# Attention output turned in 32x32 blocks on VectorE in place of TensorE transposes, in a gated cross-attention and expert kernel with a new step order

## Chip, cores and metric

One core of one Trainium2 chip. The metric is the device time of one execution in microseconds (us); lower is better. All times below are of the kernel before the change.

## The reference, cut to what matters

```python
def xattn(query, key, value):            # query = layernorm(x): 16 batches x 100 rows x 256
    Q, K, V = query @ Wq.T + bq, key @ Wk.T + bk, value @ Wv.T + bv   # key = value: 16 x 361 x 256
    # 16 heads of 16
    scores = softmax(einsum('bhsd,bhtd->bhst', Q, K) / sqrt(16))
    out = einsum('bhst,bhtd->bhsd', scores, V).reshape(B, 100, 256)
    return out @ Wh.T + bh

x = x + tanh(g_xattn) * xattn(layernorm(x), ctx, ctx)
x = x + tanh(g_ffn) * ffn(layernorm(x))  # RMS norm, gate with top 2 of 8 experts,
                                         # shared w1, w3, w2 with low-rank terms per expert
```

## The kernel before, in words

**Two phases.** The attention runs over the 16 batches in steps `i`; each `body(i)` is written out by hand once for every engine, and the engines meet only at semaphores. The expert part follows: 32 passes `g` (4 groups of 4 batches, 8 slices of 128 hidden columns). The last two attention steps, `late_step` (step 14) and `last_step` (step 15), have orders of their own, since the expert part's weights and first tokens are prepared in them. Every engine executes its list strictly in order, so a wait holds all that stands behind it in that list.

**One ordinary step, `body(i)`, on TensorE:**
- `s_head(i+1, h)`, 16 of them (L1270): scores of batch i+1 with the rows of the query on partitions, one head at a time, into two PSUM banks in turn. Each needs the maximum of head h-2 to be taken (`head`, VectorE, L985). The negated maxima go to `nmax`.
- `row_turn` and `second_rows` (L1276): the maxima of 8 heads turned to rows; ScalarE copies them to `crow` (`row_copy`, L513) and sends them (`row_send`, L517, a small DMA) into row 96 of the stack QS[b % 3]. That row, times ones in KS, subtracts the maximum inside the score matmul.
- `st_unit(i, u)`, 12 of them (L1293): transposed scores of batch i, keys on partitions, four heads in each unit, in three banks in turn; ScalarE's `expo(i, u)` (L525) takes the exponential to `pt`. Unit n needs exponential n-3. Units 0 to 5 need the first row transfer (`cr_a`), units 6 to 11 the second (`cr_b`).
- `k_part` (L1240) and `v_part` (L1252): K and V of batch i+2 as sums of high and low parts, in the two banks `pP`. ScalarE makes `k_high` and `v_out`, VectorE `k_low` (L818). SP and GpSimd send the K halves into the stacks KS (L244, L343).
- `pv_unit(i, u)`, 12 units of 4 matmuls (L1306), at the step's end: the share-weighted values and, by a column of ones in `va`, the sums. Head 4q+g goes to partitions 32g to 32g+16 and columns 100q to 100q+99 of the bank `pO`.

**What is done with `pO`, one step later.** ScalarE copies it to `osb` first thing in its `body` (L639; L681, L707 and L733 in the last steps). TensorE turns it with four 128x100 transposes (`o_turn`, L1314 to L1318) into `pP[1]`. VectorE takes the reciprocal of the sums (`shares`, L960) and multiplies (`quotient`, L966) into `on`. SP stores `on` to `o_dram` and loads it back as `xr` (L287, L294), which lays heads and rows out as the reference's reshape wants them; the bias of V goes the same way once, through `v_dram` (L290). In the next step TensorE turns `xr` (`on_turn`, L1330), VectorE copies it to `ot` (`turned_o`, L971), TensorE multiplies with Wh (`y_proj`, L1339) and VectorE adds to `xs` (`first_sum`, L976; `variance` follows, L823).

**Context.** GpSimd loads the context of batch i+4 into `craw` (`ctx_load`, L338), issues the q loads (`q_load`, L333), the low K stacks (`k_stack_low`, L343) and, after them, the low half of the context of batch i+3 (`ctx_low`, L328), for which ScalarE's `ctx_high_of(i+3)` (L471) must be done; then one of the expert weight loads (`late_load`, L354, steps 3 to 10: three of 512 KB, three of 256, one of 264, one of 128).

**Shared places.** `pP[1]` holds in turn the K half 0, `o_turn`'s result, the row turn of the first maxima, `on_turn`'s and `y_proj`'s results.

## Time and profile before

| | us |
|---|---|
| median of 3 runs | 501.02 (500.54 to 503.68) |
| the profiled execution | 504.5 |
| its span, first to last instruction | 502.6 |
| TensorE matmuls busy | 485.9 (97%) |
| TensorE weight loads busy | 455.5 (91%) |
| VectorE busy | 357.5 (71%) |
| ScalarE busy | 266.6 (53%) |
| GpSimd busy | 276.3 (55%) |

The profile is of one execution. PE is TensorE, PEld its weight loads, DVE VectorE, ACT ScalarE, POOL GpSimd, SP the engine that only issues transfers; an engine name with q behind it is that engine's issuing of DMAs. An instruction's row gives its start, duration, line, output and inputs; in brackets stands the idle time before it and what ended it. Starts of matmuls in a row show what each costs, their durations overlap.

### The profile page before, as it was taken

How to read it: one execution, taken by the hardware profiler on the slowest of the kernel's cores; microseconds unless marked ns; L12 is line 12 of the kernel's file. 1: busy time of each engine (PE TensorE's matmuls, PEld its weight loads, DVE VectorE, ACT ScalarE, POOL GpSimd, SP SyncE). 2: the span in 40 equal slices, each digit the busy share in tenths (PEclk: the TensorE clock that was granted, in tenths of full speed). 3: DMA queues.
4: the chain of work that ended last, by engine and by line, in shares of the span. 5: the costliest groups of instructions: out<-in, count | busy, mean ns of one | idle time of the engine just before them, and what ended most of it. 6: DMA issues, size and time to landing. Idle time of an engine off the chain costs nothing.

```text
span 502.6 us, 11753 instructions
## 1 busy us (share of the span) xinstructions
PE 485.9 (97%) x4350; PEld 455.5 (91%) x4350; DVE 357.5 (71%) x771; ACT 266.6 (53%) x584; POOL 276.3 (55%) x336
## 2 busy tenths in 40 slices
PE   7888999999999999999999999999999999999996
PEld 6656999999999999998999998999999999999994
DVE  6846787878778878987796879756476556764444
ACT  4446766676766666668866532534435423333331
POOL 5646555666666666566415437634396434844440
PEclk9979999999999999999999999999999999999999
DMA  6793686677767676554260000010000100001001
GB/s 204 179 291 90 198 209 150 151 202 204 199 172 177 161 168 161 126 121 94 29 206 9 1 0 2 1 34 0 1 1 1 34 1 1 0 2 34 0 1 33
DMA packets 51144, 45.83 MB, mean 91 GB/s; under 512 B 33935, under 2 KB 40115, under 8 KB 51088
## 3 DMA queue, kind: packets, MB, share of 16 engines
q1 hardware_dynamic: 41310, 23.18, 19.6%
q0 software_dynamic: 7504, 18.69, 14.1%
q10 hardware_dynamic: 2274, 3.21, 1.9%
q8 instruction: 35, 0.57, 0.5%
q14 instruction: 21, 0.17, 0.1%
HBM read 20.59 MB, written 6.66 MB: 54 GB/s over the span
## 4 chain that ended last, share of the span: by engine, by line
PE 87%; DMA 5%; DVE 4%; issue 1%; ACT 1%; POOL 1%; ACTq 0%; DVEq 0%
PE bank L1426 14%; PE bank L1270 8%; PE bank L1293 7%; PE bank L1306 7%; PE bank L1430 7%; PE bank L1443 7%; PE bank L1478 6%; PE bank L1252 6%; PE bank L1240 5%; PE bank L1458 4%; DMA QS<-crow 3%; PE bank L1339 3%; PE bank L1227 2%; PE bank L1461 2%; PE bank L1386 2%; DMA craw<-ctxT 2%
## 5 line engine op out<-in xcount | busy, mean ns | idle before, releaser
L985 DVE TENSOR_REDUCE nmax<-bank 100x1 f32<-100x361 f32 x256 | 129.9, 529 | 38.2 <-PE bank L1270 33.4
L419 POOL TENSOR_TENSOR awl<-hb,awh 128x400 fp32r<-128x400 f32 x63 | 71.2, 1132 | 119.8 <-ACT awh L623 119.8
L525 ACT ACTIVATE pt<-bank 120x400 f32<-120x400 f32 (+1 forms) x192 | 90.0, 501 | 24.1 <-PE bank L1293 11.1
L623 ACT ACTIVATE awh<-hb 128x400 fp32r<-128x400 f32 x64 | 34.5, 539 | 118.5 <-DVE hb L921 118.2
L1270 PE MATMUL bank<-KS,QS 96*100 96x362 f32 x256 | 87.0, 359 | 3.4 <-DVE nmax L985 3.1
L914 DVE TENSOR_TENSOR hb<-sil,bank 128x400 f32<-128x400 f32 x64 | 36.5, 570 | 71.4 <-PE bank L1443 36.8
L1293 PE MATMUL bank<-QS,KS 97*120 97x200 f32 (+1 forms) x384 | 66.3, 270 | 0.7 <-DMA QS<-crow 0.6
L328 POOL TENSOR_TENSOR cth<-craw,cth 128x724 fp32r<-128x724 f32 x16 | 27.6, 1728 | 64.8 <-ACT cth L471 55.2
L1293 PEld LDWEIGHTS bank<-QS,KS 97*120 97x120 f32 (+1 forms) x384 | 60.3, 184 | 1.9 <-DMA QS<-crow 1.5
L1270 PEld LDWEIGHTS bank<-KS,QS 96*100 96x100 f32 x256 | 41.7, 167 | 10.3 <-DVE nmax L985 3.7
L333 POOL DMA_DIRECT2D QS<-q_dram x90 | 46.0, 519 | 0.4 <-issue 0.3
L1252 PE MATMUL bank<-wkv,cth 128*120 128x256 f32 (+1 forms) x288 | 45.2, 286 | 0.0
L921 DVE TENSOR_TENSOR hb<-hb,wbT 128x400 f32<-128x400 f32 x64 | 43.2, 675 | 2.1
L1240 PE MATMUL bank<-cth,wkv 128*128 128x362 f32 x192 | 41.9, 330 | 0.8 <-POOL wkv L321 0.8
L343 POOL DMA_DIRECT2D KS<-kn x64 | 31.9, 508 | 16.1 <-DVE kn L818 10.4
L618 ACT ACTIVATE sil<-bank 128x400 f32<-128x400 f32 x64 | 31.5, 492 | 16.4 <-PE bank L1430 11.7
L1252 PEld LDWEIGHTS bank<-wkv,cth 128*120 128x120 f32 (+1 forms) x288 | 39.3, 183 | 0.3 <-issue 0.3
L1306 PE MATMUL bank<-pt,va 120*17 120x100 f32 (+1 forms) x1536 | 36.5, 249 | 0.0
L1306 PEld LDWEIGHTS bank<-pt,va 120*17 120x17 f32 (+1 forms) x1536 | 32.5, 97 | 3.8 <-issue 3.6
L1240 PEld LDWEIGHTS bank<-cth,wkv 128*128 128x128 f32 x192 | 32.7, 190 | 1.4 <-POOL wkv L321 1.4
L423 POOL TENSOR_TENSOR awsl<-aws,awsh 128x400 fp32r<-128x400 f32 x31 | 33.8, 1090 | 0.0
L502 ACT ACTIVATE va<-bank 120x256 f32<-120x256 f32 (+1 forms) x48 | 18.4, 383 | 8.4 <-PE bank L1252 8.2
(225 smaller groups left out, 1109.7 us busy)
## 6 DMA issues: line engine op xcount, KB each, us to landing
KS<-kn SPq DMA_DIRECT2D x128, 90.5 KB, 3.3
KS<-kn POOLq DMA_DIRECT2D x64, 90.5 KB, 3.4
craw<-ctxT POOLq DMA_DIRECT2D x14, 361.0 KB, 5.1
QS<-q_dram POOLq DMA_DIRECT2D x92, 50.0 KB, 3.5
q_dram<-qn ACTq DMA_DIRECT2D x4, 400.0 KB, 4.4
o_dram<-on SPq DMA_DIRECT2D x16, 100.0 KB
xr<-o_dram SPq DMA_DIRECT2D x16, 100.0 KB
y<-xs SPq DMA_DIRECT2D x8, 200.0 KB
```

Of the source, the lines that this page charges most:

```text
L333: pool.dma_start(QS[b % 3][row + DH * odd:row + DH * odd + DH, :, odd, :, :].rearrange("p g j s -> p g (j s)").bitcast(F32), src[odd]).the ...
L419: nc.gpsimd.tensor_tensor(awl[:, g % 2, slot], hb[:, slot], awh[:, g % 2, slot].bitcast(F32), ALU.subtract).then_inc(m["p_awl"], 1)
L525: nc.scalar.activation(pt[0:TW[t], u, :], pT[u % 3][0:TW[t], 0:CS], ACT.Exp, scale=float(DH) ** -0.5).then_inc(m["act_e"], 1)
L914: nc.vector.tensor_tensor(hb[:, slot], sil[:, slot], pU[1][:, 0:CS], ALU.mult).then_inc(m["d_hb"], 1)
L921: nc.vector.tensor_tensor(hb[:, slot], hb[:, slot], wbT[g // FT % 2][:, slot], ALU.mult).then_inc(m["d_aw"], 1)
L985: nc.vector.tensor_reduce(nmax[:, h // 8, pos % 8:pos % 8 + 1], pS[h % 2][0:S, 0:T], AX.X, ALU.max, negate=True).then_inc(m["dve_s"], 1)
L1240: last = mm(pP[(1, 0)[j]][:, 0:TP], wkv[:, 0, hw, k, j * 128:(j + 1) * 128], cth[:, b % 2, hc, k, :], start=p == 0, stop=p == 5)
L1252: last = mm(bank[0:TW[t], 0:D], cth[:, b % 2, hc, k, T0[t]:T0[t] + TW[t]], wkv[:, 1, hw, k, :], start=p == 0, stop=p == 5)
L1270: mm(pS[h % 2][0:S, 0:TP], QS[b % 3][0:96, g, h % 2, j, :], KS[b % 3][0:96, g, j, :], start=True, stop=True).then_inc(m["pe_s"], 1)
L1293: last = mm(pT[u % 3][0:TW[t], j * 2 * S:(j + 1) * 2 * S], KS[b % 3][:, q, j, T0[t]:T0[t] + TW[t]], QS[b % 3][:, q, :, j, :], start=True, ...
L1306: last = mm(pO[32 * g:32 * g + VW, q * S:(q + 1) * S], va[0:TW[t], b % 3, t, 4 * q + g, :], pt[0:TW[t], u, g * S:(g + 1) * S], start=t == ...
L1426: mm(pU[a][:, 0:CS], up_w[a][hw][:, j, fs], tt[hc][c % 2][:, j, :], start=t + j == 0, stop=False)
```

## The change

The bank `pO` is turned by one VectorE block transpose (each 32x32 block in its place) straight into `oT`: 13 blocks of 32 columns, so partitions 32g + (row in block), block c, and the 17 values of a head side by side. Head 4g+q now lies in group g. `shares` and `quotient` work on 128 partitions. `o_dram` has a layout by blocks, the loads into `xr` come in two halves (rows of even and odd start) over 104 rows, and `turned_o` puts the columns in order with two strided copies. `pO` and `xr` are filled once at the start. ScalarE's copies to `osb` and TensorE's `o_turn` are gone. The permutation of the columns of Wq and Wk follows. The order of the ordinary step and of steps 14 and 15 is new on TensorE, ScalarE and VectorE.

```diff
-        o_dram = nc.dram_tensor("o_dram", [B, H * S, DH], F32, kind="Internal").ap()
+        o_dram = nc.dram_tensor("o_dram", [B, OC, 128, DH], F32, kind="Internal").ap()      # OC = 13, RG = 26
-        osb = sba("osb", [128, NQ, S])
-        on = sba("on", [S, H, DH])
-        xr = sba("xr", [S, D])
+        oT = sba("oT", [128, OC, 32])
+        on = sba("on", [128, OC, DH])
+        xr = sba("xr", [4 * RG, D])
...
 SP, body(i)
-                    sp.dma_start(xr[:], o_dram[i - 1].rearrange("(r c) d -> r (c d)", c=H)).then_inc(m["xi"], 16)
+                    for half in range(2):
+                        sp.dma_start(xr[half * 4 * OC:(half + 1) * 4 * OC],
+                                     o_dram[i - 1].rearrange("c (g h p) d -> h g c (p d)", g=4, h=2)[half]).then_inc(m["xi"], 16)
...
 ScalarE, body(i)
-                if has_o(i):
-                    wait(act, "pe_pv", i * UN)
-                    wait(act, "pe_oT", i - 1)
-                    nc.scalar.activation(osb[:].rearrange("p q s -> p (q s)"), pO[:, 0:CS], ACT.Copy).then_inc(m["act_o"], 1)
+                if has_c(i):
+                    ctx_high_of(i + 3)
                 row_copy(i, 1)
                 row_send(i, 1)
+                k_high(b, 0)
                 expo(i, 0)
-                k_high(b, 0)
+                k_high(b, 1)
                 expo(i, 1)
-                k_high(b, 1)
                 expo(i, 2)
...
                 expo(i, 7)
+                expo(i, 8)
                 v_out(b, 1)
-                expo(i, 8)
+                row_send(i + 1, 0)
                 expo(i, 9)
-                row_send(i + 1, 0)
                 expo(i, 10)
                 expo(i, 11)
                 v_out(b, 2)
-                if has_c(i):
-                    ctx_high_of(i + 3)
...
 VectorE, start
             nc.vector.memset(nmax[:], 0.0).then_inc(m["nm_ok"], 1)
+            nc.vector.memset(pO[:, 0:OC * 32], 1.0).then_inc(m["pO_ok"], 1)
+            nc.vector.memset(xr[:], 0.0).then_inc(m["xr_ok"], 1)
...
+            def blocks_turned(i):
+                dve.wait_ge(m["pe_pv"], i * UN)
+                wait(dve, "dve_on", i - 1)
+                nc.vector.transpose(oT[:].rearrange("p c d -> p (c d)"), pO[:, 0:OC * 32]).then_inc(m["dve_o"], 1)
...
             def turned_o(i):
                 dve.wait_ge(m["pe_onT"], i)
-                nc.vector.tensor_copy(ot[:].rearrange("p k s -> p (k s)"), pP[1][:, 0:KT * S]).then_inc(m["dve_ot"], 1)
+                for half in range(2):
+                    nc.vector.tensor_copy(ot[:].rearrange("p k (g s) -> p k g s", g=4)[:, :, :, half:25:2],
+                                          pP[1][:, 0:KT * 4 * RG].rearrange("p (k h g c) -> p h k g c", k=KT, h=2, g=4)[:, half, :, :, 0:OC - half]).then_inc(m["dve_ot"], 1)
...
 VectorE, body(i)
                 head(i + 1, 0)
                 head(i + 1, 1)
+                if has_o(i):
+                    blocks_turned(i)
                 head(i + 1, 2)
...
                 k_low(b, 1)
+                head(i + 1, 6)
                 if has_o(i):
                     shares(i)
-                head(i + 1, 6)
                 head(i + 1, 7)
-                if has_o(i):
-                    quotient(i)
                 head(i + 1, 8)
                 head(i + 1, 9)
                 head(i + 1, 10)
                 head(i + 1, 11)
+                if has_o(i):
+                    quotient(i)
+                head(i + 1, 12)
+                head(i + 1, 13)
                 if has_y(i):
                     turned_o(i)
...
                 (variance and first_sum now stand here, before heads 14 and 15)
                 head(i + 1, 14)
                 head(i + 1, 15)
...
 TensorE
-            def o_turn(i):
-                ...
-                wait(pe, "act_o", i)
-                for q in range(NQ):
-                    last = nc.tensor.transpose(pP[1][0:S, q * 128:(q + 1) * 128], osb[:, q, :], ident[:])
-                last.then_inc(m["pe_oT"], 1)
...
 TensorE, body(i), b = i + 2, s = s_head(i + 1, .), st = st_unit(i, .), k and v in halves (a, b); the new order in full:
+  s0 s1 k0a k0b s2 st0 s3 k1a k1b s4 st1 s5 st2 st3 s6 st4 s7 st5 v0a st6 s8 v0b s9 row_turn st7 st8 s10
+  v1a s11 v1b st9 s12 st10 s13 st11 on_turn v2a s14 v2b s15 y_proj, then pv 0 to 11, second_rows
-  s0 st0 s1 k0a s2 k0b s3 k1a s4 st1 k1b s5 st2 o_turn st3 st4 s6 s7 st5 v0a v0b st6 s8 st7 s9 st8 row_turn
-  v1a s10 v1b on_turn s11 st9 st10 s12 v2a v2b s13 st11 y_proj s14 s15, then pv 0 to 11, second_rows
...
 late_step, last_step: o_turn out, blocks_turned in on VectorE; st_unit(B - 1, 0) and (B - 1, 1) with their
 exponentials move from last_step into late_step; on_turn(B - 1) comes first in last_step after gate(0);
 on_turn(B - 2) and y_proj(B - 2) come earlier; w_high and tokens_high on ScalarE, and masks, first_u,
 second_u, variance on VectorE, are put in a new order
```

## Rows read from the trace of the kernel before

**Rows 1.** The page, shares of the span in the chain that ended last, by engine
```profile
PE 87%; DMA 5%; DVE 4%; issue 1%; ACT 1%; POOL 1%; ACTq 0%; DVEq 0%
```
**Rows 2.** Windows by step: stretch, length, busy of PE, PEld, DVE, ACT, POOL, PEclk, DMA
```profile
178.01:191.25 13.24, 13.24 (x182) 12.57 (x186) 10.66 (x25) 8.99 (x22) 8.78 (x14) 1.00 0.74 179
...
sum 147.61, PE 146.91 PEld 138.44 DVE 118.81 ACT 99.27 POOL 94.44; mean PE 13.36 PEld 12.59 DVE 10.80 ACT 9.02 POOL 8.59
...
231.60:242.49 10.89, 10.89 (x160) 9.37 (x164) 9.46 (x24) 10.30 (x24) 7.39 (x5) 1.00 0.23 30
...
253.16:264.40 11.24, 11.24 (x150) 10.59 (x150) 10.37 (x19) 6.66 (x15) 2.67 (x2) 1.00 0.69 208
```
**Rows 3.** The chain in order of time, inside the step from 123.73
```profile
126.65 5.45 DMA QS<-crow
```
**Rows 4.** Windows, a stretch of the start
```profile
29.40:36.20 6.80, 6.46 (x14) 3.71 (x15) 1.81 (x4) 1.55 (x4) 5.04 (x10) 0.50 1.06 296
```
**Rows 5.** Timeline of TensorE in the quiet step: start, duration, line
```profile
180.14 0.25 PE L1276 MATMUL bank<-ident,nmax 100*8 100x100 f32 x1
...
181.44 0.66 PE L1240 MATMUL bank<-cth,wkv 128*128 128x362 f32 x3
181.94 0.33 PE L1270 MATMUL bank<-KS,QS 96*100 96x362 f32 x1
...
183.86 0.60 PE L1318 MATMUL bank<-ident,osb 128*100 128x128 f32 x4
184.22 0.66 PE L1293 MATMUL bank<-QS,KS 97*121 97x200 f32 x4
184.72 0.49 PE L1270 MATMUL bank<-KS,QS 96*100 96x362 f32 x2
...
185.25 0.89 PE L1252 MATMUL bank<-wkv,cth 128*121 128x256 f32 x6
185.97 0.36 PE L1293 MATMUL bank<-QS,KS 97*121 97x200 f32 x2
...
188.24 0.57 PE L1293 MATMUL bank<-QS,KS 97*121 97x200 f32 x4
188.65 0.33 PE L1270 MATMUL bank<-KS,QS 96*100 96x362 f32 x1
```
**Rows 6.** Timeline of ScalarE in the quiet step
```profile
180.27 0.50 ACT L639 ACTIVATE osb<-bank 128x400 f32<-128x400 f32 x1 [1.95 <-PE bank L1306]
...
180.93 0.63 ACTq L517 DMA_DIRECT2D QS<-crow  x1
...
182.14 0.56 ACT L496 ACTIVATE kn<-bank,bks 128x362 fp32r<-128x362 f32 x1
```
**Rows 7.** Groups by line, whole span: count | busy us, mean ns | idle before
```profile
L895 DVE TENSOR_TENSOR uth<-uTh,mk 128x800 fp32r<-128x800 f32 x4 | 6.5, 1618 | 0.1
...
L971 DVE COPY ot<-bank 128x200 f32<-128x200 f32 x17 | 6.1, 356 | 0.0
...
L950 DVE COPY fo<-bank 128x400 f32<-128x400 f32 x4 | 2.3, 575 | 2.0 <-PE bank L1514 1.7
```
**Rows 8.** Timeline of VectorE in the quiet step
```profile
182.76 0.59 DVE L818 SCALAR_TENSOR_TENSOR kn<-bank,bks,kn 128x362 fp32r<-128x362 f32 x1
...
185.08 0.97 DVE L985 TENSOR_REDUCE nmax<-bank 100x1 f32<-100x361 f32 x2
...
189.89 0.53 DVE L985 TENSOR_REDUCE nmax<-bank 100x1 f32<-100x361 f32 x1 [0.21 <-PE bank L1270]
```
**Rows 9.** Timelines of GpSimd and ScalarE at the start of step 4
```profile
112.39 0.73 POOL L354 DMA_DIRECT2D w<-w3T  x1
113.12 0.72 POOL L338 DMA_DIRECT2D craw<-ctxT  x1
...
113.22 0.63 ACTq L517 DMA_DIRECT2D QS<-crow  x1
```
**Rows 10.** Timeline of VectorE in the start
```profile
10.04 0.54 DVE L779 CAST cth<-craw 128x724 fp32r<-128x724 f32 x1 [1.76 <-DMA craw<-ctxT]
```

More of the change, by code:

```diff
@@ L1097, in late_step @@
                 head(B - 1, 6)
-                shares(B - 2)
                 head(B - 1, 7)
-                quotient(B - 2)
+                blocks_turned(B - 2)
                 head(B - 1, 8)
                 head(B - 1, 9)
+                turned_o(B - 2)
+                shares(B - 2)
+                head(B - 1, 10)
+                quotient(B - 2)
+                head(B - 1, 11)
                 tokens_low(0, 0)
-                head(B - 1, 10)
-                head(B - 1, 11)
-                turned_o(B - 2)
                 head(B - 1, 12)
@@ L1678, in late_step @@
                 st_unit(B - 2, 7)
-                on_turn(B - 2)
-                token_turn(0, 1)
+                y_proj(B - 2)
                 st_unit(B - 2, 8)
```

194 lines of the change are left out of this document (91 added, 103 removed).

## The prediction

> **What bounds the kernel.** Four views, in this order. First the shares of the chain that ended last: TensorE has 87% of it, a transfer 5%, VectorE 4% [rows 1]. So time comes off only where TensorE's own queue gets shorter or stops waiting. Second, the windows, one per ordinary step: a quiet step takes 13.24 us and TensorE is busy in all of it; VectorE has 10.66 us of work, ScalarE 8.99, GpSimd 8.78 [rows 2]. VectorE is therefore the next limit, at 81% of a step. The eleven steps from 70.20 to 217.81 sum to 147.61 us [rows 2], 1.97 more than eleven quiet ones (145.64). Third, the chain inside one of the long steps says what that excess is: TensorE waits for the small transfer that carries the negated maxima into QS (5.45 us from issue) [rows 3]. Fourth, the timelines of TensorE, VectorE and ScalarE inside the quiet step.
>
> **The profiled execution against the median.** It took 504.5 us, 502.6 of them span; the median of the runs is 501.02. The windows of the start show 6.80 us with the granted clock at 0.50, its lower level, with TensorE busy 6.46 us of them [rows 4]; at full clock that work would need about half, 3.2 us. That is nearly the whole difference of 3.5 us, so I take the median to be the same program without that stretch, work out differences in the profiled step and subtract them from 501.02.
>
> **Removed on TensorE: `o_turn`.** In the quiet step its four transposes start at 183.86 and the score units behind them at 184.22, so 0.36 us. Those four score matmuls then run to 184.72, 0.50 us, where the same four elsewhere need 188.24 to 188.65, 0.41 [rows 5]. The 0.09 more is the tail of the transposes. Price of one `o_turn`: 0.45 us. There are 16.
>
> **Removed on ScalarE: the copy to `osb`.** It starts at 180.27, and the send of the maxima is issued at 180.93, holding ScalarE 0.63 us [rows 6]. Without the copy the row copy starts when its transpose is done, about 0.24 us earlier, and so does the send.
>
> **Added on VectorE.** The block transpose, 416 elements from PSUM into SBUF. No such operation is in the trace. Nearest from below is the 128x200 copy at 356 ns; a copy of 128x400 from PSUM takes 575; the dearest pass over a similar tile is 1618 ns for 128x800 [rows 7]. I take 0.58, nearest in shape and source, and keep 0.36 and 1.62. The Trainium skill, "Vector Engine (DVE) Microarchitecture Reference", section 3.8, says the reorder array passes one element per cycle and lane when it transposes; with a clock of 0.96 GHz that is an estimate of 0.43 us for the stream alone, and no run here shows it yet. The reciprocal shrinks from 16 to 13 columns a partition and the quotient from 256 to 208: nothing much. `turned_o` becomes two strided copies of 104 and 96 columns for one of 200: between 0 and 0.36 more, I take 0.15. Together VectorE gets 0.6 to 0.7 us more a step, 11.3 of 13.
>
> **The new order of an ordinary step,** walked from its start R (the transpose of the second maxima), with starts from the timelines: a score head takes 0.17 us, a score unit 0.20, half a K projection 0.50 (181.44 to 181.94), half a V projection 0.36 (185.25 to 185.97 is two) [rows 5]; VectorE starts heads 0.44 apart when they wait for nothing (two in 0.97, one lasting 0.53), and a `k_low`, 0.59 long, holds it 0.5 by the same overlap [rows 8]. R is 180.14 in the quiet step.
> - The transpose sits behind head 1, from R+1.33. Head 2 comes only after a whole K projection, with its maximum ready to start at R+1.79, and head 4 at R+3.34, so the transpose is hidden up to about 0.7 us of duration. It costs TensorE nothing at 0.58. Behind it on VectorE queue all heads, and TensorE's heads wait two heads back, so beyond 0.7 us everything shifts.
> - K high 1 on ScalarE (0.56 us [rows 6]) now stands before exponential 1; its projection's last matmul starts before R+2.97, and 0.3 later its bank can be read, so it ends at R+3.83 and frees ScalarE 0.09 before that. Exponential 1 ends at 4.24, and score unit 4, which needs its bank, would start at 4.09: 0.18 late. Unit 5 is 0.07 late behind exponential 2. Head 9 needs maximum 7, which VectorE ends at R+5.95: TensorE is there at 5.95 by then. So some 0.27 us of waits, at one place.
> - Further on nothing waits by more than 0.05. The order of now has some 0.1 us of small gaps of its own, around `y_proj` and the last two heads (an estimate: what the quiet step's 13.24 has over the sum of its parts at these spacings); heads 14 and 15 now stand ahead of `y_proj`, so I let them go.
> Sum: 13.24 - 0.45 + 0.27 - 0.10 = 12.96, so 0.28 less, 13 steps: **3.6 us**.
>
> **The transfer of the maxima.** Two changes pull against each other. Score unit 6, which waits for the second half, moves up from R+5.83 to R+5.27, while the send moves up only by 0.24; In the quiet step the send is issued at R+0.79; with the 5.45 us of the long step it lands at R+6.24 now and at R+6.00 after, and unit 6 would wait 0.7 us for it. But what stands ahead of it moves too: GpSimd issues a 512 KB weight load at 112.39 and the 361 KB context load at 113.12, just as the maxima are sent at 113.22 in that step [rows 9]. In the new order ScalarE makes the high half of the context one batch ahead, so GpSimd's `ctx_low` no longer waits for it; it runs after the K low stacks, and the two big loads leave about 3.5 us before R. The maxima then find the queues emptier. From 164.78 on, where those loads are small or over, the same transfer lands in time already. I count 1.6 of the 1.97 us as gained: **1.6 us**.
>
> **Steps 14 and 15 and the first expert pass** hold three more `o_turn`, 1.35 us. Step 14 (231.60 to 242.49) is 10.89 us with VectorE at 9.46 and ScalarE at 10.30 [rows 2]; there the transpose isn't hidden and two exponentials and two score units of step 15 come in, which step 15 loses again. I take 0.5 off: **0.85 us**. In the expert pass (253.16 to 264.40) the transpose delays VectorE's products by 0.5, but TensorE is busy in all 11.24 us of it [rows 2], so it has work in hand: nothing, at worst 0.5. **Start:** two memsets more on VectorE, which later sits idle 1.76 us for the first context [rows 10]: nothing; at worst 0.7, since a tile of 400 columns costs 0.58 [rows 7] and the other memset is smaller. **SP:** eight small loads of `xr` in step 0 in place of one, and two a step after; all are issued in stretches in which SP has only its waits: nothing. The quotient comes later (after head 11), and its store still leaves behind the K stacks as now: `on_turn` of the next step waits for neither.
>
> **Total:** 3.6 + 1.6 + 0.85 = 6.05. From the profiled execution 504.5 - 6.05 = 498.45; from the median 501.02 - 6.05 = 495.0.
>
> **Rivals.**
> - *Clean gain.* TensorE waits nowhere new: 16 x 0.45 + 1.97 + 13 x 0.05 = 9.8, so 491.2. For it: ScalarE and VectorE are not full. Against: the waits above come out of the order itself. Chance 0.15.
> - *VectorE takes over in the first half of the step.* Each of its operations would hold it for longer than the heads' spacing shows, for instance the transpose and the two strided copies by 0.3 us more each way; ordinary steps then gain only about 0.05: 495.0 + 13 x 0.23 + 0.5 = 498.5. Against it: heads that last 0.53 us start 0.44 apart [rows 8]. Chance 0.13. The Trainium skill, "VectorE: DVE Perf Modes", section "The DRAIN you can't avoid", states that after every operation the pipeline is flushed for about its duration less 266 ns, and advises to keep the number of operations low; by that rule a transpose of 0.58 would hold VectorE for 0.89, and the trace disagrees, since a head is followed by the next before its own end.
> - *The maxima land too late.* If their transfer keeps its 5.45 us, unit 6 waits 0.7 in the six steps with a weight load: 495.0 + 6 x 0.7 + 0.3 = 499.5. For it: the unit moved up more than the send. Chance 0.14.
> - *The block transpose is dear, and the kernel slower.* Place: behind head 1, with all of the step's maxima behind it. Up to 0.7 us it is free, and above that each 0.1 us costs 0.1 in 13 ordinary steps and 2 others. The 6.05 are used up at 0.7 + 6.05/15 = 1.1 us. At 1.62 us [rows 7] it is 495.0 + 15 x 0.92 = 508.8. For it: it moves data across lanes, and none of the rows does. Chance 0.08.
> - *The change doesn't do what it says,* the reordering giving as much away as `o_turn` frees: 501 less the transfers, 499 to 501. It is in the chances of the second and third rivals.
>
> **How the numbers follow.** The forecast, with its own range 493 to 498, has 0.50. About 1% (5 us) is what a measurement of this kernel tells from no change. Faster by more (below 496.0): most of the forecast's 0.50 (0.42) and the clean gain's 0.15, 0.57. Slower (above 506.0): most of the last case, 0.08. Between: 0.35. The range reaches from 490.5, a little under the clean gain, to 501.0, which holds the second and third rivals and leaves the dear transpose out.
>
> **What would show it.** A block transpose of 0.5 to 0.65 us; L1318 gone; quiet steps near 12.96; the step's first waits on TensorE at score units 4 and 5 for ScalarE; no or hardly a wait for the maxima's transfer in the chain, GpSimd's context load before R; VectorE near 11.3 us a step. It is wrong if quiet steps stay at 13.2 (then look at VectorE between heads 4 and 9), if the transfer's share of the chain stays at 3% or more, or if the transpose lasts over 0.7 us. The clock may also fall elsewhere in the start, which is worth up to 3 us in a single run and nothing on the change.

## The result and the profile after

The changed kernel takes 511.88 us (median, 510.03 to 514.25) against 502.31 us for the kernel before on the same chip (500.54 to 503.68): ratio 1.0199, 95% interval 1.0161 to 1.0238. The forecast was 495.0 us, in a range of 490.5 to 501.0; the time came out 16.9 us above it, and slower than before. The profiled execution took 511.96 us, 510.2 of them span. Here and below a ratio counts only executions in the chip's faster state while a median counts all of them, which matters for two of the runs.

The page of the kernel after: busy times, and the chain that ended last by engine and by line.
```profile
PE 485.0 (95%) x4286; PEld 450.4 (88%) x4286; DVE 373.6 (73%) x806; ACT 253.5 (50%) x568; POOL 276.1 (54%) x336
...
PE 79%; DVE 14%; issue 3%; ACT 2%; DMA 1%; DVEq 0%; ACTq 0%
```
TensorE's share of the chain fell from 87% to 79% and VectorE's rose from 4% to 14%; the transfers went from 5% to 1% [rows 1]. So the transfers did leave the chain, as forecast, and VectorE took their place.

Windows of the kernel after, by step, with the columns of rows 2. Each window begins at the first product of probabilities and values, which closes one step, and is named here after the step that follows it; the last two rows are steps 12 and 13.
```profile
83.15:97.10 13.95, 13.46 (x175) 12.31 (x174) 11.81 (x26) 8.16 (x21) 8.58 (x15) 1.00 0.70 173
...
180.73:194.68 13.95, 13.48 (x175) 12.32 (x174) 11.79 (x26) 8.15 (x21) 8.23 (x14) 1.00 0.70 160
...
208.62:223.09 14.47, 13.70 (x176) 12.37 (x175) 13.21 (x33) 7.52 (x20) 7.55 (x13) 1.00 0.52 116
223.09:238.21 15.12, 13.72 (x177) 12.71 (x177) 14.08 (x33) 8.30 (x21) 6.18 (x11) 1.00 0.46 104
```
The ten ordinary steps from 69.23 to 208.62 are all alike, 13.92 to 13.95 us, where the quiet one was 13.24 [rows 2]. The eleven from 69.23 to 223.09 add up to 153.86 us, 6.25 more than the 147.61 before. TensorE is no longer busy in all of a step: 13.48 of 13.95.

Where in the step it is lost, the timelines of VectorE, GpSimd and TensorE say (start, duration, line; three fences, one engine each).
```profile
176.09 1.06 DVE L988 TENSOR_REDUCE nmax<-bank 100x1 f32<-100x361 f32 x2
177.06 1.35 DVE L967 TENSOR_TENSOR on<-oT,rz 128x208 f32<-128x208 f32 x1
178.34 0.96 DVE L988 TENSOR_REDUCE nmax<-bank 100x1 f32<-100x361 f32 x2
```
```profile
176.41 1.76 POOL L337 TENSOR_TENSOR cth<-craw,cth 128x724 fp32r<-128x724 f32 x1
178.09 0.56 POOL L363 DMA_DIRECT2D ag<-agT  x1
```
```profile
178.92 0.41 PE L1280 MATMUL bank<-KS,QS 96*100 96x362 f32 x1 [0.49 <-DVE nmax L988]
```
The quotient lasts 1.35 us and ends at 178.41, just after GpSimd's `ctx_low` (to 178.17). The maxima of heads 12 and 13 come behind it, and TensorE waits for them at head 14. The groups by tile say that this is the rule.
```profile
L958 DVE STREAM_TRANSPOSE oT<-bank x16: 605/606/616, 58.4 to 266.7; 128x416 f32<-128x416 f32 x16
L962 DVE RECIPROCAL rz<-oT x16: 220/230/241, 62.2 to 267.3; 128x13 f32<-128x13 f32 x16
L967 DVE TENSOR_TENSOR on<-oT,rz x16: 355/1349/1376, 66.4 to 267.6; 128x208 f32<-128x208 f32 x16
```
Minimum, median and maximum in ns: the quotient needs 355 where GpSimd computes nothing beside it, and 1349 in the median. The block transpose is 606 ns, as forecast.

The last steps lose in the same way. VectorE in steps 13 and 15 of the kernel after, and GpSimd beside the second group:
```profile
223.60 0.77 DVE L842 SCALAR_TENSOR_TENSOR rt<-rt,scl 100x8 f32<-100x8 f32 x1
224.40 0.65 DVE L844 SCALAR_TENSOR_TENSOR scl<-rt,scl 100x8 f32<-100x8 f32 x1
...
253.31 0.98 DVE L967 TENSOR_TENSOR on<-oT,rz 128x208 f32<-128x208 f32 x1
...
255.03 1.52 DVE L866 TENSOR_TENSOR dm<-top 100x4 f32<-100x4 f32 x1
```
```profile
252.76 1.30 POOL L411 TENSOR_TENSOR a2l<-a,a2h 128x512 fp32r<-128x512 f32 x1 [0.75 <-ACT a2h L599]
254.01 2.51 POOL L411 TENSOR_TENSOR w2l<-w,w2h 128x1024 fp32r<-128x1024 f32 x1
```
A multiplication of 100x8 takes 0.77 us and a difference of 100x4 1.52. Two windows, the first of the kernel after, the second of the kernel before, show what stands behind the last product's start:
```profile
259.11:505.46 246.35, 243.53 (x1463) 235.48 (x1462) 162.16 (x303) 98.64 (x201) 121.11 (x103) 1.00 0.05 17
```
```profile
253.09:497.87 244.78, 243.25 (x1467) 235.98 (x1466) 160.34 (x297) 99.11 (x203) 121.86 (x103) 1.00 0.05 16
```
That is 1.57 us more. With the eleven steps (+6.25), the start and first step (-0.97) and the three steps between (+0.7) it makes the 7.6 us by which TensorE ends later in the two profiled executions (505.46 against 497.87). The medians lie 9.6 apart. Most of the rest is the clock in the start: the profiled execution of before has 6.8 us at the granted clock of 0.50 there [rows 4], that of after 3.4 (30.30 to 33.71), and half of the difference, 1.7 us, is my estimate of what that lent the kernel after; so the -0.97 isn't a gain of the change.

### The profile page after: what moved, and what is told of

It reads as the page before. It is cut to its first block, busy times and chain, and to the rows that moved or that the text cites. A ratio compares the mean times of both kernels' runs of the same rounds, so it can differ in the third digit from the quotient of the medians.

```text
span 510.2 us, 11653 instructions
## 1 busy us (share of the span) xinstructions
PE 485.0 (95%) x4286; PEld 450.4 (88%) x4286; DVE 373.6 (73%) x806; ACT 253.5 (50%) x568; POOL 276.1 (54%) x336
## 4 chain that ended last, share of the span: by engine, by line
PE 79%; DVE 14%; issue 3%; ACT 2%; DMA 1%; DVEq 0%; ACTq 0%
PE bank L1425 13%; PE bank L1280 8%; PE bank L1429 6%; PE bank L1477 6%; PE bank L1303 6%; PE bank L1442 6%; PE bank L1316 6%; PE bank L1250 5%; PE bank L1262 4%; PE bank L1457 4%; DVE nmax L988 3%; DVE on L967 3%; PE bank L1338 3%; PE bank L1237 3%; PE bank L1460 2%
## 5 line engine op out<-in xcount | busy, mean ns | idle before, releaser
L988 DVE TENSOR_REDUCE nmax<-bank 100x1 f32<-100x361 f32 x256 | 126.8, 521 | 22.2 <-PE bank L1280 19.1
L534 ACT ACTIVATE pt<-bank 120x400 f32<-120x400 f32 (+1 forms) x192 | 83.9, 504 | 6.5 <-PE bank L1303 6.5
L1303 PE MATMUL bank<-QS,KS 97*120 97x200 f32 (+1 forms) x384 | 68.0, 273 | 1.0 <-DMA QS<-crow 1.0
L1303 PEld LDWEIGHTS bank<-QS,KS 97*120 97x120 f32 (+1 forms) x384 | 58.4, 184 | 3.7 <-DMA QS<-crow 1.2
L1262 PE MATMUL bank<-wkv,cth 128*120 128x256 f32 (+1 forms) x288 | 50.9, 289 | 0.0
L919 DVE TENSOR_TENSOR hb<-hb,wbT 128x400 f32<-128x400 f32 x64 | 44.3, 692 | 2.1
L1262 PEld LDWEIGHTS bank<-wkv,cth 128*120 128x120 f32 (+1 forms) x288 | 42.3, 182 | 0.5 <-issue 0.3
L1250 PE MATMUL bank<-cth,wkv 128*128 128x362 f32 x192 | 37.4, 330 | 0.0
L505 ACT ACTIVATE kn<-bank,bks 128x362 fp32r<-128x362 f32 x32 | 17.9, 562 | 24.4 <-PE bank L1250 24.4
```

Source lines behind the costliest of these rows:

```text
L534: nc.scalar.activation(pt[0:TW[t], u, :], pT[u % 3][0:TW[t], 0:CS], ACT.Exp, scale=float(DH) ** -0.5).then_inc(m["act_e"], 1)
L919: nc.vector.tensor_tensor(hb[:, slot], hb[:, slot], wbT[g // FT % 2][:, slot], ALU.mult).then_inc(m["d_aw"], 1)
L988: nc.vector.tensor_reduce(nmax[:, h // 8, pos % 8:pos % 8 + 1], pS[h % 2][0:S, 0:T], AX.X, ALU.max, negate=True).then_inc(m["dve_s"], 1)
L1250: last = mm(pP[(1, 0)[j]][:, 0:TP], wkv[:, 0, hw, k, j * 128:(j + 1) * 128], cth[:, b % 2, hc, k, :], start=p == 0, stop=p == 5)
L1262: last = mm(bank[0:TW[t], 0:D], cth[:, b % 2, hc, k, T0[t]:T0[t] + TW[t]], wkv[:, 1, hw, k, :], start=p == 0, stop=p == 5)
L1303: last = mm(pT[u % 3][0:TW[t], j * 2 * S:(j + 1) * 2 * S], KS[b % 3][:, q, j, T0[t]:T0[t] + TW[t]], QS[b % 3][:, q, :, j, :], start=True, ...
```

## The experiments

Theory A, from these rows: VectorE's operation with SBUF operands only is held while GpSimd reads SBUF; the quotient came into that place because its input moved from PSUM to SBUF, and because `ctx_low` and the quotient now fall together. Rival: the quotient is slow by itself (its strided view of 13 groups of columns, or the order it stands in). The Trainium skill, "SBUF — State Buffer", section "🔬 SBUF: two separate sides", states the rule: VectorE and GpSimd share a pair of ports under an exclusive lock, a VectorE operation with two SBUF inputs competes for it with a GpSimd operation that reads SBUF, and whichever starts first holds it for its whole instruction while the other waits. By that rule the quotient would end after `ctx_low`, which the rows above show (178.41 and 178.17).

**Take the overlap away, in three ways.** GpSimd's low half before its stacks of k; the quotient behind head 7; ScalarE's high half back at the end of its step.
```diff
 # e1_low_first, GpSimd
+                if i >= -1 and has_c(i):
+                    ctx_low(i + 3)
                 if i >= 0 and has_k(i):
...
                     k_stack_low(i + 2)
-                if i >= -1 and has_c(i):
-                    ctx_low(i + 3)
 # e2_quotient_early, VectorE
                 head(i + 1, 7)
+                if has_o(i):
+                    quotient(i)
...
                 head(i + 1, 11)
-                if has_o(i):
-                    quotient(i)
 # e3_high_back, ScalarE
-                if has_c(i):
-                    ctx_high_of(i + 3)
                 row_copy(i, 1)
...
                 v_out(b, 2)
+                if has_c(i):
+                    ctx_high_of(i + 3)
```


> Only edit to the changed kernel: GpSimd makes the low half of the context (ctx_low, 1.76 us) before the K low stacks of the same step, so at about 1 to 3 us of the step in place of 7.4 to 9.2, where VectorE's quotient stands. Theory A (the quotient, whose two inputs now both lie in SBUF, is held while that GpSimd pass runs): the quotient falls from 1.35 us to 0.36 in every step, quiet steps from 13.94 to 12.9 to 13.0, the whole from 511.9 by 11 to 12 us to about 500. Rival B (the quotient is slow by itself where it stands, or VectorE is simply full in the new order, so that another operation takes its place as the last one): quiet steps stay at 13.7 or more, the whole above 508.

> Only edit to the changed kernel: VectorE's quotient stands behind head 7 in place of head 11; GpSimd's queue is as in the changed kernel, so at that time it issues the K low stacks and the low half of the context has not begun. Theory A: the quotient takes 0.36 us there, although GpSimd issues transfers beside it; it adds 0.3 us to the maxima that bind between heads 7 and 9, so quiet steps come to 13.0 to 13.3 and the whole to 500 to 504. Rival B (any work of GpSimd beside it, issuing transfers too, holds it): it stays above 0.8 us, quiet steps stay at 13.7 or more, the whole above 508.

> Only edit to the changed kernel: ScalarE makes the high half of the context at the end of the step and not one batch ahead, as in the kernel before. GpSimd's low half then waits for it and runs at the end of the step, and the weight and context loads stand beside the send of the maxima again. Theory A: the quotient takes 0.36 us; quiet steps (with small loads) about 12.95. For the maxima's transfer I expect TensorE to wait for it in the steps 3 to 7, by 0.3 to 0.7 us each, so the whole is 2 to 4 us above the run with the low half first: 502 to 504. Rival B: quotient 1.35, the whole above 508. If the transfer wait is absent, the whole equals that of the run with the low half first within 1 us.

Measured: 519.9 us (ratio 1.0346, 1.0285 to 1.0407), 510.31 (1.018, 1.0126 to 1.0233) and 520.32 (1.0351, 1.029 to 1.0412). The quotient's group in the second, then its longest one:
```profile
L967 DVE TENSOR_TENSOR on<-oT,rz x16: 353/359/2429, 62.7 to 265.6; 128x208 f32<-128x208 f32 x16
```
```profile
132.14 2.43 DVE L967 TENSOR_TENSOR on<-oT,rz 128x208 f32<-128x208 f32 x1 [1.19 <-DMA o_dram<-on]
```
In all three the median is 0.36 or 0.37 us and an undisturbed step 13.09 to 13.17. The hold is gone from the ordinary step, theory A stands for the quotient and its rival falls. The one long quotient of the second run says the same: it came late, since it had to wait for the store before it, fell beside `ctx_low` (132.61 to 134.33) and lasted until 134.57. But the time didn't come back. My totals (500, 500 to 504, 502 to 504) missed by 6 us and more and lie where I had put the rival, and two of the runs are slower than the changed kernel. Who waits for a transfer, and windows of the first:
```profile
PE bank L1329 <- DMA xr<-o_dram: 7.5, 5, 2.4
```
```profile
170.41 8.20 DMA o_dram<-on
```
```profile
169.70:187.07 17.37, 14.48 (x175) 12.79 (x174) 10.91 (x26) 8.29 (x21) 12.18 (x20) 0.94 0.90 176
```
and of the third:
```profile
PEld bank L1303 <- DMA QS<-crow: 6.0, 5, 2.0
```
```profile
110.14:128.43 18.29, 16.47 (x176) 15.37 (x175) 11.10 (x26) 8.32 (x21) 8.92 (x14) 0.81 0.64 140
```
TensorE waits five times for `xr` in the first run, where the store of the quotient takes 7 to 9.4 us to land before the longest waits, and five times for the maxima in the third. In a step like the last row the granted clock falls to 0.81 in the mean: 18.29 us are 13.1 plus 1.8 of waiting plus 3.4, which is half of a stretch of 6.8 us at the lower level, 1.2 GHz, that follows the wait. Theory B, then: with steps of 13.1 us two transfers come too late where GpSimd's large loads (weights and context) are issued ahead of them, and a wait of TensorE can cost a stretch at 1.2 GHz besides. That the held quotient hid this, since steps of 13.94 us leave the transfers more time, is my reading and no run tests it alone; in the last run of this document, with steps of 13.94 us too, TensorE still waits twice for `xr` (3.1 us).

**A control in the kernel before**, for the other side of theory A: same collision, but the quotient reads PSUM.
```diff
 # e5_psum_beside: the kernel before
             def body(i):
                 b = i + 2
+                if has_c(i):
+                    ctx_high_of(i + 3)
...
                 v_out(b, 2)
-                if has_c(i):
-                    ctx_high_of(i + 3)
 # VectorE
                 head(i + 1, 7)
-                if has_o(i):
-                    quotient(i)
                 head(i + 1, 8)
                 head(i + 1, 9)
+                if has_o(i):
+                    quotient(i)
```


> A control in the kernel before, for the duration of one instruction and not for the time: ScalarE makes the high half of the context one batch ahead, so GpSimd's low half follows the K low stacks, and VectorE's quotient (here with one input in PSUM, one in SBUF) stands behind head 9, where that GpSimd pass runs. Theory A (only an operation whose two tensor inputs are both in SBUF is held): the quotient keeps its 0.41 us in all steps although GpSimd's pass lies over it. Rival (any VectorE operation that touches SBUF is held): 1 us or more in the steps where they overlap.

VectorE and GpSimd in that run:
```profile
62.98 0.41 DVE L966 TENSOR_TENSOR on<-bank,rz 100x256 f32<-100x256 f32 x1
```
```profile
62.84 1.74 POOL L328 TENSOR_TENSOR cth<-craw,cth 128x724 fp32r<-128x724 f32 x1
```
All 16 quotients take 0.41 or 0.42 us. But the control is weaker than planned: in 11 of the 13 steps in which the two overlap, the quotient starts 0.08 to 0.13 us ahead of `ctx_low`, where being first could save it anyway. Only this one and the one at 256.51 start inside GpSimd's operation, and they aren't held. The kernel before has the case more often, at the end of its steps (GpSimd, then VectorE):
```profile
178.41 1.72 POOL L328 TENSOR_TENSOR cth<-craw,cth 128x724 fp32r<-128x724 f32 x1 [4.13 <-ACT cth L471]
```
```profile
178.78 0.47 DVE L976 SCALAR_TENSOR_TENSOR xs<-bank,tgx,xs 100x256 f32<-100x256 f32 x1
179.17 0.42 DVE L823 BATCH_NORM_STATS2 stats<-xs 100x6 f32<-100x256 f32 x1
```
`first_sum`, with one input in PSUM, starts inside `ctx_low` in eleven steps and takes 0.47 or 0.48 us each time. So an operation with an input in PSUM isn't held. The second row narrows theory A: `variance` reads and writes SBUF only, with one tensor as input, and keeps its 0.42 us inside `ctx_low` as well. SBUF operands only are not enough; the quotient has two SBUF inputs. The total (513.89 us, one run) says nothing on this: TensorE's turn of the maxima stands earlier in that order, needs the bank that the quotient reads, and waits for it 13 times, 10.8 us in all.

**Only the transpose moved, all orders as before.**
```diff
 # e4_old_order: the changed kernel with the bodies of the kernel before
                 head(i + 1, 1)
+                if has_o(i):
+                    blocks_turned(i)
...
-                if has_o(i):
-                    o_turn(i)             # TensorE
```


> The changed kernel with the ordinary step's orders of the kernel before on TensorE, ScalarE and VectorE; the block transpose stands behind head 1, o_turn and the copy to osb are gone; steps 14 and 15 are those of the change. Theory A: the old order has neither the collision (GpSimd's low half runs at the step's end, the quotient behind head 7) nor TensorE's waits for exponentials; quiet steps 13.24 - 0.45 = 12.8 to 12.9, some wait for the maxima's transfer in steps 3 to 7, the whole 499 to 501: so the transpose on VectorE alone is a gain and the new order alone is the loss. Rival B (the transpose on VectorE itself costs what it frees): quiet steps 13.2 or more, the whole 505 or more.

Measured: 505.62 us (1.0079, 1.0048 to 1.0109). Quiet steps are 13.12 to 13.16, so of the 0.45 us of `o_turn` only 0.1 stays, even without any new order. And two steps lose all of it again (the windows, then the chain inside them):
```profile
93.16:110.10 16.94, 14.93 (x175) 13.43 (x175) 10.81 (x27) 8.99 (x21) 9.21 (x15) 0.90 0.80 161
110.10:128.39 18.29, 16.38 (x176) 15.15 (x175) 11.00 (x27) 8.34 (x20) 8.63 (x14) 0.81 0.62 143
```
```profile
96.24 8.81 DMA xr<-o_dram
112.86 7.21 DMA QS<-crow
```
This order is 6.3 us better than the change's in the median, and still 0.8% slower than the kernel before. By its total (I had expected 499 to 501) the rival, a transpose on VectorE that costs what it frees, comes nearer than my theory; but in the profiled execution (509.17 us) the two steps with a late transfer take 9 us more than quiet ones.

**Where the loads are issued.** First the weight loads were put off to the last steps, in three kernels: the order of the first run, the old order with the block transpose, and the kernel before itself.
```diff
 # e7_loads_late, e8_old_order_loads_late, e9_before_loads_late: GpSimd
-                if 0 <= i - 3 < len(late):
-                    late_load(i - 3)
+                for n in {11: (0, 1), 12: (2, 3, 4, 5), 13: (6, 7)}.get(i, ()):
+                    late_load(n)
```


> The run with the low half first, and the eight weight loads of steps 3 to 10 issued in steps 11 to 13, where no or nearly no context load is left (two, four, two). Theory C (the quotient was only the first cause; with it gone the transfers through o_dram and the maxima come late because the weight and context loads are issued in front of them, and TensorE, after waiting some 2 us for one, gets half its clock for 3.4 or 6.8 us): steps 3 to 10 fall from 13.1 to 17.4 us to 13.1 to 13.2, no stretch of half clock stands inside them, the whole 501 to 504 (against 519.9). Rival D (the reordered queue of GpSimd, with the q loads and the context load before the step, delays them in any case, or the half clock has another cause): waits for xr or the maxima and half clock stay in at least three steps between 4 and 11, the whole above 510.

> The run with the ordinary step's old order and the block transpose, with the same weight loads moved to steps 11 to 13. Theory C: steps 1 to 11 all take 13.1 to 13.2, half clock only at start and end, the whole 497 to 500, faster than the kernel before by 0.5 to 1%. Rival D: it stays at 504 to 506.

> The kernel before with only the weight loads moved to steps 11 to 13. Theory C: the excess of its long steps (13.4 to 13.8 against 13.24) goes, some 1.5 to 2 us: 500 to 501 against 501.8. Rival D: no change or longer, since steps 11 to 13 now carry the loads.

Measured: 519.86 us (1.0373, 1.0325 to 1.0421), 509.25 (1.019, 1.0144 to 1.0237) and 509.16 (1.0178, 1.0135 to 1.022). I had expected 501 to 504, 497 to 500 and 500 to 501. In the kernel before the steps without a weight load became quiet (twelve of 13.23 to 13.44). In the other two most did, but steps of 14.08 and 14.55 in the first and three of 13.52 to 13.64 in the second remain, with small waits for `xr` or the maxima, so the weight loads were not the only ones in the way. The last steps lost more than was gained. Windows of the third, its step 13 and a part of it:
```profile
214.90:234.00 19.10, 15.89 (x163) 13.97 (x155) 12.13 (x28) 9.08 (x22) 12.01 (x22) 0.91 0.87 177
225.90:229.30 3.40, 3.25 (x15) 3.28 (x16) 1.34 (x3) 1.01 (x2) 1.03 (x2) 0.50 1.05 213
```
There TensorE waits 2.7 us for `xr`. So the kernel before has the same weak point: eight loads in three steps cost it 8 us. In the first run another thing comes on top, in VectorE's root of the variances for the expert part:
```profile
209.06 3.51 DVE L844 SCALAR_TENSOR_TENSOR scl<-rt,scl 100x8 f32<-100x8 f32 x1
```
An operation of 0.17 us lasts 3.51 here; TensorE waits 2.6 us for the maximum behind it and then has 10.2 us at the granted clock of 0.50. That step takes 20.10 us, and this isn't the loads' doing. Still, the loads don't gain anything late; they have to go elsewhere within each step. In the next two runs they leave 3 to 4 us behind the step's first product of probabilities and values, right behind the maxima and some 8 us before the store.
```diff
 # e10_loads_mid (on e1_low_first), e11_old_order_mid (on e4_old_order): GpSimd
-                if i >= -1 and i + 4 < B:
+                if -1 <= i <= 0:
                     ctx_load(i + 4)
...
                 ctx_low(i + 3)
+                if 0 <= i - 3 < len(late):
+                    late_load(i - 3)
+                if i >= 0 and i + 5 < B:
+                    ctx_load(i + 5)
                 k_stack_low(i + 2)
-                if 0 <= i - 3 < len(late):
-                    late_load(i - 3)
```


> The changed kernel with GpSimd's body in the order: sum, low half of the context, weight load, context load of the step after next (one step earlier than before), low stacks of k. Theory C (the quotient's hold by GpSimd's low half was the first loss; what then stands in the way is the round trip through o_dram and the transfer of the maxima, which come late when the large loads are issued right ahead of them, and each long wait of TensorE is followed by a stretch of half clock): the loads now start some 2.5 us into the step, after the maxima have gone and long before the store of the output, so the ordinary steps are 13.1 to 13.2 us nearly throughout, the quotient about 0.36 us, hardly a half clock stretch between 50 and 480 us, total 500 to 503 us. Rival (it is the volume of the loads, not where in a step they are issued): some steps stay at 14 to 17 us with xr or QS waits, total 515 to 520 us as in the two earlier variants of this order.

> The kernel before's order of the ordinary steps on TensorE, ScalarE and VectorE with the block transpose behind head 1 in place of the 4 TensorE transposes, the high half of the context at the front of ScalarE's step, and GpSimd's order: sum, low half, weight load, context load, low stacks. Theory C: all ordinary steps 13.1 to 13.2 us, no step of 17 or 18 us, total 499 to 502 us, that is 4 to 6 us under the old order with the loads where they were (505.6). Rival (old order is held by something else than the place of the loads): steps 6 and 7 stay at 17 to 18 us, total 505 to 509 us.

Measured: 508.17 us (1.0147, 1.0103 to 1.0191) and 516.86 (1.0316, 1.0281 to 1.0351), where I had expected 500 to 503 and 499 to 502. In the first, nine of the ten steps up to 201 are 13.10 to 13.16 us, and the store lands after 5.5 us at the latest; its median is 11.7 us under that of the same order with the loads at the end, so it isn't their volume alone. The second is a miss: its step is otherwise arranged (`ctx_high` at the front of ScalarE's old order, and GpSimd's low half moved ahead of the stacks), and TensorE still waits there for `xr` (2.5 us) and for VectorE's maxima (3.9); why is open. The first isn't done either, at 508. Its windows and timelines show why (VectorE, then GpSimd):
```profile
188.13:201.23 13.10, 13.10 (x176) 12.29 (x175) 10.79 (x26) 8.13 (x21) 7.97 (x14) 1.00 0.68 143
201.23:217.31 16.08, 13.35 (x175) 12.35 (x175) 14.68 (x33) 7.58 (x20) 7.45 (x13) 1.00 0.47 104
```
```profile
201.93 3.06 DVE L836 TENSOR_SCALAR gi<-tmpv 100x8 int32<-100x8 int32 x1
```
```profile
202.55 0.75 POOL L393 TENSOR_TENSOR xs<-xs,tbh 100x256 f32<-100x256 f32 x1
203.24 1.72 POOL L337 TENSOR_TENSOR cth<-craw,cth 128x724 fp32r<-128x724 f32 x1
```
A shift of 100x8 integers, 0.17 us elsewhere, lasts 3.06 us, through two operations of GpSimd (to 204.96). It starts 0.62 us before the first of them, while GpSimd still issues its q loads; the 3.51 us above start 1.07 us before, and the late quotient of 2.43 us 0.47 before. Why a hold can begin ahead of GpSimd's operation stays open. The shift stands ahead of heads 14 and 15, and TensorE waits 2.7 us.

**The last two places.** The root's 13 small operations, one each behind heads 4 to 10 of steps 11 and 12; then also `variance(12)`, `variance(13)` and the last batch's transpose, reciprocal and quotient behind the first products of the expert pass; and the roots alone, in the changed kernel.
```diff
 # e13_roots_moved (on e10_loads_mid), e15_after_roots (on the changed kernel)
                 head(i + 1, 4)            # and 5 to 10 alike
+                if i in (11, 12):
+                    root(0, (0, 7)[i - 11] + 0)
 # e14_pass_start (on e13_roots_moved)
                 gated(g, 0)
-                if g == 0:
-                    blocks_turned(B); shares(B); quotient(B)
                 weighted(g, 0)
+                if g == 0:
+                    blocks_turned(B); shares(B); quotient(B)
...
                     summed(g)
+                if g == 0:
+                    variance(12); variance(13)       # out of last_step
```


> The run with the loads issued in mid-step (508.2 us), with the 13 small operations of the root of group 0 moved: one each behind heads 4 to 10 of steps 11 and 12, where GpSimd reads nothing, in place of before and behind heads 14 and 15. There the integer shift of 100x8 took 3.06 us and the last steps were 16.1 and 15.4 us. Theory (an operation of VectorE with SBUF operands alone is held while GpSimd's additions and its low half run, whatever its size): each of the 13 takes 0.16 to 0.2 us, the step before the late step's is 13.1 to 13.5 us in place of 16.1, total 504.5 to 506 us. Rival (the long step is a late transfer, and the held shift lay inside it): step still above 15 us, total within 1 us of 508.

> The run above, with variance(12) and (13) behind the first expert pass, and block transpose, reciprocal and quotient of the last image behind weighted(0,0). Theory: these 1.2 us each stood ahead of gated(0,0) and weighted(0,0) on VectorE, so the distance from the last probability-value product to the end of TensorE falls from 246.3 to 245.0 to 245.6 us, total 0.7 to 1.3 us less than the run above. Rival (that distance is set by the last store's round trip or by the masks ahead of them): within 0.3 us, or longer where xr is then waited for.

> The changed kernel with the roots moved in the same way and nothing else. Its quotients stay held at 1.35 us. Theory: only steps 14 and 15 change, by 1.0 to 1.7 us in all (14.47 and 15.12 towards 13.9 and 14.6), total 510 to 511 us against 511.9. If the total falls by over 3 us, the roots' place weighed more than the trace of the changed kernel shows.

Measured: 503.29 us (1.003, 0.9992 to 1.0068; one of its ten executions took 935.74 us, and without it the median is 503.27), 501.05 (0.9989, 0.996 to 1.0017) and 511.24 (1.0195, 1.0144 to 1.0246). The same shift, and steps 11 and 12, in the first:
```profile
193.97 0.16 DVE L836 TENSOR_SCALAR gi<-tmpv 100x8 int32<-100x8 int32 x1
```
```profile
187.49:200.74 13.25, 13.25 (x175) 12.32 (x174) 11.14 (x33) 8.13 (x21) 7.98 (x14) 1.00 0.63 137
200.74:214.03 13.29, 13.29 (x176) 12.36 (x176) 11.15 (x32) 7.61 (x20) 7.51 (x13) 1.00 0.57 126
```
16.08 us became 13.29 and the 15.38 of the next step 13.41, nearly all of the 4.9 us by which the median fell, so the rival (a late transfer) falls. The profiled execution has no wait of TensorE over 0.8 us after 50 us. In the second, the stretch behind the last product is shorter:
```profile
249.42:494.97 245.55, 243.44 (x1463) 235.46 (x1462) 162.07 (x303) 98.59 (x201) 121.27 (x103) 1.00 0.06 17
```
245.55 in place of 246.32, and the median falls by 2.2 us, more than the 0.8 of this stretch explain; the two kernels' runs overlap, so only the 0.8 is shown. With it the kernel is level with the one before, 10.8 us under the changed kernel's median, the computation being the same. Nothing I ran beats the kernel before by more than its interval. In the changed kernel itself the same move lowers the median by only 0.6 us, less than the spread of its executions. The profiled one shows more: steps 12 and 13 take 14.09 and 13.45 in place of 14.47 and 15.12, but one moved operation of the root, at 208.78, now falls beside `ctx_low` (208.66 to 210.42) and lasts 1.67 us, and the step before grows from 13.93 to 14.70. That leaves 1.3 us of gain, within the 1.0 to 1.7 that I had expected.

**Another order at the end, a miss.** On the second mid-step kernel, the index ahead of the last quotient, and `variance(12)` and `(13)` behind the first expert pass.
```diff
 # e12_last_step (on e11_old_order_mid): VectorE
                 logits(0)
-                quotient(B - 1)
                 best_two(0)
+                quotient(B - 1)
```


> The run above, with best_two(0) ahead of the last quotient and variance(12) and (13) moved behind the first expert pass. Theory: the last step's VectorE chain (quotient 0.98 and dm 1.52 ahead of the index, both held beside GpSimd's low halves) made the first index turn and the masks 1 to 1.5 us late; with the order changed the stretch from the last probability-value product to the last instruction of TensorE is 1.0 to 1.5 us shorter than in the run above, total 1 to 1.5 us less. Rival (the last step's order is hidden behind TensorE's expert work): within 0.3 us of the run above.

Measured: 516.6 us (ratio 1.0218, 1.013 to 1.0306; the kernel it builds on 516.86, 1.0316, 1.0281 to 1.0351). The intervals overlap, so the totals say nothing. In the profiled execution (517.6 us) the stretch behind the last product is 250.4 us against 246.5, longer by 4 and not shorter by 1.0 to 1.5. The chain of waits in the first expert passes:
```profile
268.87 7.53 DMA o_dram<-on
...
276.42 0.68 SPq L302
...
277.14 2.77 DMA xr<-o_dram
```
The last store was issued at 268.87, 1.1 us behind SP's last weight load, and took 7.53 us. In the kernel it builds on the gap is 6.1 us, in the first run with the loads in mid-step 6.3, and TensorE doesn't wait in either. What is gained on VectorE is lost to a store behind large loads: it fits theory B, at a place where I had not looked for it, on one profiled execution.

**Is VectorE's room what the prediction said?** The block transpose twice in each step, the second behind the first.
```diff
 # e6_turned_twice (on e10_loads_mid)
+                nc.vector.transpose(oT, pO[:, 0:OC * 32]).then_inc(m["dve_oo"], 1)
+                dve.wait_ge(m["dve_oo"], i)
                 nc.vector.transpose(oT, pO[:, 0:OC * 32]).then_inc(m["dve_o"], 1)
```


> The first run of this call, with the block transpose done twice in every step, the second waiting for the first (0.61 us more of VectorE, in line). Theory of the prediction (VectorE has up to 0.7 us of room behind head 1, beyond it each microsecond is paid in full): since the one block transpose of 0.61 us has used nearly all of that room, each ordinary step grows by 0.45 to 0.65 us, some 6 to 9 us in all. Rival (the scores and score copies behind it still have slack): steps grow by under 0.15 us, total within 2 us of the first run.

Measured: 514.2 us (1.0247, 1.022 to 1.0274), 6.0 over the kernel it builds on. A step of it:
```profile
193.89:207.54 13.65, 13.49 (x175) 12.30 (x175) 11.32 (x27) 8.40 (x21) 7.96 (x14) 1.00 0.60 126
```
0.62 us more of VectorE make a step 0.53 to 0.55 longer. So the first transpose leaves under 0.1 us of room, where the prediction had 0.12 (0.7 less 0.58; with the measured 0.61 it is 0.09), and beyond it the price is in full, as it said.

## Why the prediction was wrong

- **The failed step** is the one sentence on the quotient: "The reciprocal shrinks from 16 to 13 columns a partition and the quotient from 256 to 208: nothing much." Alone it is 0.36 us, smaller than before. But the change takes its input from PSUM to SBUF, and the same order that frees `ctx_low` from its wait, which I counted only as a gain for the loads, sets that operation beside it. An ordinary step is 13.94 with it and 13.12 without; ten of them make 8.2 us, the largest part of the 9.6 us by which the kernel got slower.
- **The trace of before had shown it.** `uth` stands there with a mean of 1618 ns over four operations [rows 7], one of which (at 253.77) takes 0.99; the other three take 1.82 or 1.83, and GpSimd computes beside them. I took the mean as the price of a pass over such a tile, a bound for the transpose, and didn't ask whether it was held.
- **Right:** the block transpose, 0.606 us (0.58 taken); `turned_o` 0.41 for both copies (0.36 for one before, so +0.05, I took 0.15); its room behind head 1; `o_turn` gone; the maxima's transfer out of the chain (5% to 1%), though in steps made longer by another cause. The dear transpose, the only case in which I had "slower", was not what happened: it had the sign by luck, with another mechanism.
- **Too high: the gain of an ordinary step.** Without the hold it is 13.12, a gain of 0.12 and not 0.28. Of the 0.45 us of `o_turn`, 0.33 don't come back, and the old order gives the same 13.13, so it isn't the new order. TensorE counts as busy through all of such a step, and no run takes this apart.
- **Wrong: "nothing" for SP and the quotient's store.** `on_turn` doesn't wait for the store, but `xr` does, and that round trip (up to 9.4 us for the store alone) is the next thing to be late once steps are short. The "1.6 us" for the maxima is there in that TensorE waits only 1.0 us for them in all of the changed kernel; but I also assumed that the loads only had to be away from R; in the run with `ctx_high` put back the maxima cost 6.0 us of waits.
- **Missed: steps 12 to 14 and the expert pass** (0.85 gain and "nothing, at worst 0.5"): the root's operations, `dm` and the quotient were held there too (`dm` had 1.21 us before already), +0.6 us in step 13 and +1.57 behind the last product. Of the 1.57, moving what VectorE did there gave back 0.8; that the hold makes up the rest isn't shown. Steps 14 and 15, counted from product to product, take 20.9 us together against 20.8 before, so the 0.85 didn't come at all.
- *VectorE takes over* was the nearest rival: right engine, wrong place and size. It had 0.23 us a step; it was 0.98, from one operation and not from all.

## What to carry to other kernels

When a change moves an operand of VectorE from PSUM to SBUF, or moves such an operation in the order, list what GpSimd does at that moment: an operation with SBUF inputs only, above all one with two, can last as long as GpSimd's, whatever its own size. When a stall goes, ask which transfers it gave time to, and keep large loads away from the small store and the small row on which TensorE waits. When the minimum and the maximum of one group of equal operations lie a factor of three apart, look at what ran beside the long ones before taking the mean as a price.

## What the runs showed of the hardware

- A held VectorE operation doesn't pay a share, it pays the rest of GpSimd's: 1.35 for 0.36 us against a low half of 1.76, and 3.06 for 0.17 across two GpSimd operations in a row. The 3.06 us are also more than the two operations, by the 0.62 us ahead of them.
- With an input in PSUM nothing was held: 0.41 us for the quotient, 0.47 for `first_sum` eleven times inside `ctx_low`. Nor was every operation on SBUF alone: the statistics of `variance` kept 0.42 us beside `ctx_low`, and the reciprocal of the kernel after, at 253.04 inside GpSimd's `a2l` (252.76 to 254.06), its 0.23, while the quotient right behind it took 0.98. The statistics and the reciprocal have one SBUF input, the quotient two.
- The shift has one SBUF input too, and was held. The Trainium skill, "SBUF — State Buffer", section "🔬 SBUF: two separate sides", counts VectorE's two-port modes among the cases, so it agrees if this shift runs in one, which no row shows.
- The same store landed after 2.6 us at the least and after 9.4 at the most; with the loads in mid-step it never took over 5.5.
- After long waits of TensorE the granted clock mostly fell to 0.50, for 3.4 to 10.2 us. In the run with the low half first, waits of 2.4 and 2.7 us had 3.4 us of it behind them each, and four of 0.9 to 1.4 us had none. Not always: a wait of 2.7 us at 203.5 in the run with the loads in mid-step was followed by none, and with the transpose doubled the same wait was followed by 3.4 us of it. Over all the profiled executions, between 50 us and 480 us, it followed or met 16 of the 18 longest waits (1.8 to 3.9 us). What decides it stays open.
